# One transformer block on one core: memory rows four to a partition, the router's two halves stacked, and pieces of work put in other places

## The chip, the cores and the metric

The kernel runs on one core of a Trainium2 chip. The metric is the device time of one execution in microseconds (us). Shown are the median, lowest and highest of three executions, and one further execution that the hardware profiler recorded.

## The reference

2048 tokens (32 sequences of 64) of 256 features pass through a gated cross-attention and then a gated mixture of 8 experts with a shared expert.

```python
x = x + tanh(g_xattn) * xattn(layernorm(x), ctx, wq, wk, wv, wo)   # keys and values: [ctx, x], 64 + 64 rows per sequence
x = x + tanh(g_ffn) * ffn(layernorm(x))

def ffn(x):
    probs = softmax(x @ gate_w.T)                    # 8 experts
    top_p, top_i = top_k(probs, 2)                   # combine[n, e] = top_p where chosen, else 0
    h = silu(x @ expert_fc1[e].T) * (x @ expert_fc2[e].T)         # 176 wide, for every expert e
    y = sum_e combine[n, e] * (h @ expert_proj[e].T)
    s = silu(x @ shared_fc1.T) * (x @ shared_fc2.T)               # 704 wide
    return y + sigmoid(x @ shared_gate_w.T) * (s @ shared_proj.T)
```

## The kernel before, in words

TensorE, VectorE, ScalarE, GpSimd and the sync engine (PE, DVE, ACT, POOL and SP in the rows) each run one instruction stream in the order in which the program is written; semaphores tie them together. An engine that waits for one semaphore holds up everything behind it. Nothing but the written order sets the order of the work.

Precision: each float32 value v is kept as a rounded part "hi" (written by ScalarE, line 807, helper `copy`) and a remainder "lo" (VectorE, line 1060 or 1098, helpers `sub` and `scalar_tensor_tensor`); GpSimd makes the lo parts of some loaded data (lines 1554, 1591). A product is three matmuls: hi·hi, hi·lo and lo·hi (`THREE`, helper `chain`, line 424).

Stage by stage:

1. **Attention, chunks c = 0 to 3** of 512 tokens, each in four tiles j of 128. TensorE transposes the normed rows (`first_norm`, L432), makes queries and keys (`project(c, i)`, i = 0..3), `scores(c, j)`, `values(c, j)`, transposes the softmax (`probs_t`, L509) and multiplies (`attend(c, j)`). While chunk c is worked on, TensorE also projects chunk c+1 and norms, transposes and routes chunk c-1: `second_norm`, `router` (logits for 8 experts and the shared gate: 6 matmuls with 72 columns of weights and 512 tokens, rows "router_hi", "router_lo"), `logits` (four small transposes, L552). VectorE does `row_max`, `v_lo`, `probs_lo`, `residual` (L1131, L1135), `aggregate` (L1141) and, two chunks behind, the routing: `two_best`, `counts`, `slots` (L1222 to L1227: which slot of its expert each token takes). `route(c-2)` (L567) is the TensorE product that `slots` reads, in PSUM bank 7. In chunks 2 and 3 `slots(c-2)` stands on VectorE between `residual(c, 0)` and `v_lo(c, 1)`.
2. GpSimd `scatter(c, i)` (L1564, L1568) writes each token's normed row, in groups of 128, to its two slots in memory (`xs_d`); it also computes the reciprocal deviations (`rstd1`, `rstd2`) and the lo parts of the shared weights, after which SP loads the next piece.
3. **Shared expert** in blocks `fc(s, j)` and `pj(s, j)` (L689), s = chunk, j = 0..5. PRE = 3 chunks run before the routed experts, the last chunk after them. VectorE scales each chunk's result by its gate (`s_sums`, L1437) into the tile SX2, and SP stores it in memory (`y2_d`). The last chunk's result is added to the output by L1440.
4. **Routed experts**, 39 slot tiles of 128 rows: `e_step(s, u, m)`, 2 us each. TensorE transposes (L740, L784) and multiplies; GpSimd adds each tile's rows to their tokens' rows in `y2_d` with an indirect, accumulating DMA (L1608).
5. **Combine** (L1402): SP reads the two sums of every token back from `y2_d` (L403, eight loads of 512 KB into the tile called ew_hi), VectorE adds them, SP and ScalarE store the output.

At the start SP issues, in this order: x of chunk 0, the attention weights (3 loads), the context `ctx_t[0]`, x of chunk 1; then, once GpSimd has made the lo part of the context (`cached_lo(0)`, L1554), the next context, constants, and x of chunk 2 (L293). On ScalarE `cached_hi(0)`, which waits for the context, stands ahead of `weight_hi(2)`, `weight_hi(3)`, `project_hi(0, ..)` and `first_apply(1)` (L839), and this last waits for GpSimd's `rstd1(1)`, which stands behind `cached_lo(0)`. VectorE's `ln1_stats(c)` (L1071) waits for x of chunk c; `ln1_stats(2)` stands ahead of `v_lo(0, 0)`. TensorE runs 18 transposes of a constant whose results nobody reads (`warm`, L579), once the constants have come (`d_const`).

## Time and profile before

| | |
|---|---|
| three executions: median (lowest to highest) | 299.07 us (297.09 to 299.75) |
| the profiled execution: its time, its span | 299.84 us, 298.03 us (the page shows 298.0) |
| busy: TensorE, VectorE, ScalarE, GpSimd | 276.6, 215.6, 170.2, 130.3 us |
| chain that ended last | TensorE 59%, VectorE 19%, issue 8%, ScalarE 7%, DMA 4% |
| mean granted TensorE clock | 0.990 of 2.4 GHz |

The busy time of TensorE counts pipelined matmuls up to their modelled ends, so neighbours overlap: the starts in the timeline tell more than the durations. Brackets at the end of a row give the idle time of its engine just before it and what ended that. The chain of waits goes from the last instruction back to what released each step; work that stands in it can't be made longer without a later end.

### The profile page before, as it was taken

How to read it: one execution, taken by the hardware profiler on the slowest of the kernel's cores; microseconds unless marked ns; L12 is line 12 of the kernel's file. 1: busy time of each engine (PE TensorE's matmuls, PEld its weight loads, DVE VectorE, ACT ScalarE, POOL GpSimd, SP SyncE). 2: the span in 40 equal slices, each digit the busy share in tenths (PEclk: the TensorE clock that was granted, in tenths of full speed). 3: DMA queues.
4: the chain of work that ended last, by engine and by line, in shares of the span. 5: the costliest groups of instructions: out<-in, count | busy, mean ns of one | idle time of the engine just before them, and what ended most of it. 6: DMA issues, size and time to landing. Idle time of an engine off the chain costs nothing.

```text
span 298.0 us, 5868 instructions
## 1 busy us (share of the span) xinstructions
PE 276.6 (93%) x1785; PEld 247.8 (83%) x1785; DVE 215.6 (72%) x700; ACT 170.2 (57%) x399; POOL 130.3 (44%) x157
## 2 busy tenths in 40 slices
PE   4988899999999899999999999799999999999991
PEld 3877789789779587798788888699999999998881
DVE  6667776879869748767776767877777787763285
ACT  2766678687566347574235455366676667654230
POOL 2330831542784525445550000057777787775000
PEclk9999999999999799999999999999999999999998
DMA  7470244221135202544415654358888888856796
GB/s 212 164 244 9 71 133 152 70 74 53 47 96 221 79 34 73 187 129 142 142 62 176 218 183 143 108 105 139 132 141 135 141 133 141 119 68 70 257 354 236
DMA packets 30654, 40.18 MB, mean 135 GB/s; under 512 B 2976, under 2 KB 26656, under 8 KB 30624
## 3 DMA queue, kind: packets, MB, share of 16 engines
q1 hardware_dynamic: 22480, 29.53, 31.5%
q0 software_dynamic: 7152, 9.57, 19.5%
q10 hardware_dynamic: 992, 0.71, 0.8%
q8 instruction: 15, 0.25, 0.4%
q14 instruction: 15, 0.12, 0.1%
HBM read 22.68 MB, written 17.11 MB: 134 GB/s over the span
## 4 chain that ended last, share of the span: by engine, by line
PE 59%; DVE 19%; issue 8%; ACT 7%; DMA 4%; POOL 1%; SPq 0%; DVEq 0%; ACTq 0%; POOLq 0%
PE bank L424 45%; PE bank L689 7%; DVE ew_lo L1060 4%; DMA xn_all<-x_dram 3%; ACT ew_hi L807 3%; PE bank L784 3%; PE bank L740 3%; DVE xt_lo L1060 2%; DVE work L1415 2%; DVE neg_max L1108 2%; ACT sh_hi L807 1%; DMA weight_stage<-ew_dram 1%; ACT work L839 1%; DVE work L1437 1%; DVE ln_stats L1071 1%
## 5 line engine op out<-in xcount | busy, mean ns | idle before, releaser
L1608 POOL DMA_INDIRECT y_d<-work,dest_of_slot x39 | 60.5, 1552 | 57.1 <-DVE dest_of_slot L1461 55.6
L424 PE MATMUL bank<-ew_hi,xt_hi 128*128 (+2 forms) x172 | 53.8, 322 | 1.1 <-DVE xt_lo L1060 0.6
L424 PE MATMUL bank<-ew_lo,xt_hi 128*128 (+2 forms) x172 | 51.8, 301 | 0.0
L424 PE MATMUL bank<-ew_hi,xt_lo 128*128 (+1 forms) x133 | 40.5, 305 | 0.0
L1060 DVE TENSOR_TENSOR xt_lo<-bank,xt_hi 128x256 fp32r<-128x256 f32 (+2 forms) x90 | 35.6, 398 | 2.8 <-ACT xt_hi L807 1.5
L1568 POOL DMA_INDIRECT xs_d<-xn_all,slot_of_pair x32 | 33.0, 1032 | 10.1 <-issue 7.3
L424 PE MATMUL bank<-xt_hi,sw_hi 128*128 128x512 f32 x88 | 34.8, 396 | 0.2 <-issue 0.2
L807 ACT ACTIVATE xt_hi<-bank 128x256 fp32r<-128x256 f32 (+1 forms) x90 | 32.8, 409 | 3.4 <-PE bank L784 2.2
L424 PE MATMUL bank<-xt_lo,sw_hi 128*128 128x512 f32 x88 | 34.5, 392 | 0.0
L424 PE MATMUL bank<-xt_hi,sw_lo 128*128 128x512 f32 x88 | 34.3, 390 | 0.0
L1060 DVE TENSOR_TENSOR ew_lo<-bank,ew_hi 128x512 fp32r<-128x512 f32 (+1 forms) x41 | 22.7, 582 | 15.9 <-ACT ew_hi L807 13.8
L424 PEld LDWEIGHTS bank<-ew_hi,xt_hi 128*128 128x128 f32 (+1 forms) x172 | 32.5, 189 | 1.8 <-issue 0.9
L424 PE MATMUL bank<-ew_hi 128*128 128x256 f32 (+1 forms) x100 | 30.9, 315 | 3.2 <-DVE ew_lo L1060 1.8
L424 PEld LDWEIGHTS bank<-ew_lo,xt_hi 128*128 128x128 f32 (+1 forms) x172 | 32.8, 191 | 0.2
L424 PE MATMUL bank<-ew_hi,ew_lo 128*128 128x256 f32 (+1 forms) x100 | 30.6, 312 | 1.5 <-DVE ew_lo L1060 1.5
L807 ACT ACTIVATE sh_hi<-work 128x512 fp32r<-128x512 f32 (+1 forms) x24 | 15.2, 632 | 28.1 <-DVE work L1415 17.9
L424 PE MATMUL bank<-ew_lo,ew_hi 128*128 128x256 f32 (+1 forms) x100 | 30.0, 306 | 1.2 <-DVE ew_lo L1280 0.6
L689 PE MATMUL bank<-sw_hi,sh_hi 128*128 128x256 f32 x96 | 27.1, 288 | 2.2 <-DVE sh_hi L1060 1.9
L807 ACT ACTIVATE ew_hi<-bank 128x512 fp32r<-128x512 f32 (+1 forms) x45 | 21.6, 518 | 9.7 <-PE bank L424 8.2
L689 PE MATMUL bank<-sw_lo,sh_hi 128*128 128x256 f32 x96 | 26.6, 282 | 0.0
L424 PEld LDWEIGHTS bank<-ew_hi,xt_lo 128*128 128x128 f32 x133 | 25.0, 188 | 0.0
L1447 DVE TENSOR_TENSOR work<-work,bank 128x176 f32<-128x176 f32 x39 | 13.1, 337 | 15.5 <-ACT work L1002 15.5
(161 smaller groups left out, 680.9 us busy)
## 6 DMA issues: line engine op xcount, KB each, us to landing
work<-xs_d SPq DMA_DIRECT2D x39, 136.0 KB
weight_stage<-ew_dram SPq DMA_DIRECT2D x10, 486.5 KB, 3.8
ew_hi<-y_d SPq DMA_DIRECT2D x8, 512.0 KB, 7.4
y_d<-work SPq DMA_DIRECT2D x6, 512.0 KB, 3.7
work<-ctx_t_dram SPq DMA_DIRECT2D x4, 512.0 KB, 3.6
xn_all<-x_dram SPq DMA_DIRECT2D x3, 512.0 KB, 6.4
xs_d<-pad_row SPq DMA_DIRECT2D x9, 136.0 KB, 1.9
weight_stage<-sw_dram SPq DMA_DIRECT2D x3, 384.0 KB
```

The lines of the kernel that those rows point to most:

```text
L424: last = nc.tensor.matmul(dst, a, b, start=(n == 0), stop=(n == len(pairs) - 1))
L689: last = nc.tensor.matmul(B[4 + t][:, 0:D], h[:, t * P:(t + 1) * P], w, start=(j == 0 and n == 0), stop=(j == S_FULL and n == len(parts) - 1))
L740: last = nc.tensor.transpose(rows_bank(n)[:, k * P:(k + 1) * P], EX[:, w, k * P:(k + 1) * P], ident)
L784: last = nc.tensor.transpose(B[4 + v][:, i * P:(i + 1) * P], EH[:, v, i * P:(i + 1) * P], ident)
L807: return nc.scalar.activation(dst, src, ACT.Copy, scale=scale)
L839: nc.scalar.activation(XA[:, j, :], XNR[:, c * TPC + j, :], ACT.Identity, bias=nb1[:, j:j + 1], scale=rs1[:, j:j + 1]).then_inc(a_xn, 1)
L1060: return nc.vector.tensor_tensor(dst, src, hi.bitcast(F32), ALU.subtract)
L1108: last = nc.vector.tensor_reduce(nmx[r, j % 2:j % 2 + 1], own_keys(B[4 + j % 2], b), mybir.AxisListType.XY, ALU.max, negate=True)
L1415: nc.vector.tensor_tensor(SHF[0:rows, j % 2, :], STH[0:rows, j % 2, :], h2, ALU.mult).then_inc(v_h, 1)
L1447: nc.vector.tensor_tensor(EH[:, u % 2, 0:F_E], ETH[:, u % 2, :], B[2 + u % 2][:, F_E:2 * F_E], ALU.mult)
L1568: nc.gpsimd.indirect_dma_start(out=xs_d, out_offset=bass.IndirectOffsetOnAxis(ap=POS[:, i, n:n + 1], axis=0), in_=XN[:, n, :], in_offset=N ...
L1608: nc.gpsimd.indirect_dma_start(out=y2_d, out_offset=bass.IndirectOffsetOnAxis(ap=IX[:, n:n + 1], axis=0), in_=EY[:, n % 4, :], in_offset=None,
```

## The change

- **Rows in memory.** The sums in `y2_d` lie four tokens to a partition (token row = 512 c + 4 p + j), so a partition's four rows are one stretch of 4 KB; the slots' destinations (the table `C_TOK`) follow.
- **Router.** Hi and lo weights stand side by side in one tile `router` (columns 0 to 8 and 32 to 40), so one pass gives both products: 4 matmuls instead of 6, with lo·lo added. The logits are transposed with 41 rows instead of 9, and VectorE's copy becomes a sum over the two halves (L1151 before).
- **Routing's slots.** On VectorE `slots(c-2)` goes behind `aggregate(c, 0)`; on TensorE `route(c-2)` goes behind `attend(c, 1)`, into bank 4, and `attend(c, 1)` no longer waits for `v_pos`. On GpSimd `rstd2(c, 0)` goes ahead of the scatter, and the second scatter of chunk 0 into chunk 3.
- **Start.** x of chunk 1 is issued ahead of the context. `ln1_stats(2)` goes behind `row_max(0, 2)`; `project_lo(1, 0)` ahead of `residual(0, 0)`; `project_lo(0, 0)` behind `weight_lo(3)`. The 18 empty transposes become 30 empty matmuls of 64 columns, of which 22 wait only for the memset of `pad_row`.
- **Chunk 1.** `scores(1, 0)` stands between the two halves of `first_norm(2)`. **Chunk 2.** `project(3, 3)` stands ahead of `attend(2, 2)`, on VectorE alike.
- **Before the expert steps.** Of the four products of `s_sums(2)` VectorE does the first ahead of the steps and the second within step 0; ScalarE does the third and fourth within step 0.
- **Last chunk.** `fc(3, 5)` goes ahead of `pj(3, 3)`; `combine(5)` between `s_mult(3, 5)` and `s_lo(3, 5)`, `combine(4)` likewise in block 4. Four of the eight loads from `y2_d` are issued by ScalarE.

```diff
-        y2_t = y2_d[0:TOP * N_TOK, :].rearrange("(i c j p) d -> i c p j d", i=TOP, c=N_CH, j=TPC)
+        y2_t = y2_d[0:TOP * N_TOK, :].rearrange("(i c p j) d -> i c p j d", i=TOP, c=N_CH, j=TPC)
...
-        RW = [sb(f"router_{s}", [P, KD, RW_COLS], F32R) for s in ("hi", "lo")]
+        RW = sb("router", [P, KD, RW_COLS], F32R)
...
+            load_x(1)
             sp.dma_start(CR, ctx_t[0]).then_inc(d_ct, 16)
-            load_x(1)
...
-                sp.wait_ge(v_z, 4 * s + 4)
+                sp.wait_ge(v_z, 4 * s + 4 if s < PRE - 1 else 4 * s + 2)
+                if s == PRE - 1:
+                    sp.wait_ge(a_z, 2)
...
             for c in LAST_FIRST:
-                for i in range(TOP):
-                    sp.dma_start(Y2[i][:, c * TPC:(c + 1) * TPC, :], y2_t[i, c]).then_inc(d_y[i][c], 16)
...
+                    if c > 2:
+                        waits += [(0, v_pos, c - 2)]
...
-                if j == 1 and c > 1:
-                    waits = waits + [(0, v_pos, c - 1)]
...
-                             [(RW[a][:, k, :], XT[b][:, c, k, :]) for k in range(KD) for a, b in THREE], waits)
+                             [(RW[:, k, :], XT[b][:, c, k, :]) for k in range(KD) for b in range(2)], waits)
...
-                    last = nc.tensor.transpose(B[7][:, j * 16:j * 16 + N_E + 1], LGT[:, j * P:(j + 1) * P],
-                                               ident[0:N_E + 1, 0:N_E + 1])
+                    last = nc.tensor.transpose(B[7][:, j * 2 * RW_LO:j * 2 * RW_LO + RW_ROWS], LGT[:, j * P:(j + 1) * P],
+                                               ident[0:RW_ROWS, 0:RW_ROWS])
...
-                bank, o = (B[1], 0) if c == LAST else (B[7], D)
+                bank, o = (B[1], 0) if c == LAST else (B[7], D) if c == LAST - 1 else (B[4], 0)
...
                 else:
-                    pe.wait_ge(v_x2, 4 * (c + 2))
+                    pe.wait_ge(a_exp, 4 * (c + 2) + 3)
...
                 for _ in range(n):
-                    nc.tensor.transpose(B[5][:, 0:P], ident, ident)
...
 
+            pe.wait_ge(zeroed, 1)
+            warm(22)
             pe.wait_ge(d_const, 16)
-            warm(10)
             first_norm(0, 0)
-            warm(4)
             first_norm(0, 1)
-            warm(4)
...
-                if 0 < c < LAST:
+                if c == 1:
                     first_norm(c + 1, 0)
+                    scores(c, 0)
                     first_norm(c + 1, 1)
-                scores(c, 0)
-                scores(c, 1)
+                    scores(c, 1)
+                else:
+                    if c < LAST:
+                        first_norm(c + 1, 0)
+                        first_norm(c + 1, 1)
+                    scores(c, 0)
+                    scores(c, 1)
                 values(c, 0)
...
-                if c > 1:
-                    route(c - 2)
...
                 attend(c, 1)
+                if c > 1:
+                    route(c - 2)
...
-                attend(c, 2)
+                if c != LAST - 1:
+                    attend(c, 2)
                 values(c, 3)
                 probs_t(c, 3)
                 if c < LAST:
                     project(c + 1, 3)
-                else:
+                if c == LAST - 1:
+                    attend(c, 2)
+                if c == LAST:
...
+                    if (s, j) == (PRE - 1, S_FULL) and t < TPC - 1:
+                        last.then_inc(p_pre, 1)
...
-                if s == 1:
-                    pe.wait_ge(v_z, 4 * PRE)
+                if s in (1, 2):
+                    pe.wait_ge(v_z, 4 * (PRE - 1) + s)
+                if s in (2, 3):
+                    pe.wait_ge(a_z, s - 1)
...
-            blocks(PRE, N_CH, 1)
+            fc(LAST, 1)
+            for j in range(2, S_BLK):
+                if j < S_FULL:
+                    pj(LAST, j - 2)
+                fc(LAST, j)
+            for j in range(S_FULL - 2, S_BLK):
+                pj(LAST, j)
...
+                if s == 0:
+                    act.wait_ge(d_z, 16 * (PRE - 1))
+                    for t in (2, 3):
+                        T = (PRE - 1) * TPC + t
+                        if t == 2:
+                            act.wait_ge(p_pre, 3)
+                        else:
+                            act.wait_ge(p_pj, 6 * PRE)
+                        copy(SX2[:, t, :], B[4 + t][:, 0:D], scale=GS[:, T:T + 1]).then_inc(a_z, 1)
...
+                s_hi(LAST, j)
+                if j == 1:
+                    for r in range(4):
+                        act.wait_ge(d_ey[r], 16 * len(range(r, SLOT_TILES, 4)))
+                if j in (1, 2):
+                    for c in LAST_FIRST[2 * j - 2:2 * j]:
+                        act.dma_start(Y2[1][:, c * TPC:(c + 1) * TPC, :], y2_t[1, c]).then_inc(d_y[1][c], 16)
             at = (LAST - 1) * TPC + 2
...
-                nc.vector.tensor_copy(LG[:, c * TPC:(c + 1) * TPC, :],
-                                      B[7][:, 0:TPC * 16].rearrange("p (j n) -> p j n", j=TPC)[:, :, 0:N_E + 1]).then_inc(v_lg, 1)
+                both = B[7][:, 0:TPC * 2 * RW_LO].rearrange("p (j x n) -> p j n x", j=TPC, x=2)[:, :, 0:N_E + 1, :]
+                nc.vector.reduce_sum(LG[:, c * TPC:(c + 1) * TPC, :], both, AX_X).then_inc(v_lg, 1)
...
-            project_lo(0, 0)
             weight_lo(2)
             weight_lo(3)
+            project_lo(0, 0)
...
 
             row_max(0, 0)
...
+            ln1_stats(2)
             v_lo(0, 1)
             probs_lo(0, 1)
+            project_lo(1, 0)
             residual(0, 0)
-            project_lo(1, 0)
...
-                if c > 1:
-                    slots(c - 2)
                 v_lo(c, 1)
...
                 aggregate(c, 0)
                 if c + 2 < N_CH:
                     ln1_stats(c + 2)
+                if c > 1:
+                    slots(c - 2)
...
-                residual(c, 2)
+                if c != LAST - 1:
+                    residual(c, 2)
                 v_lo(c, 3)
                 probs_lo(c, 3)
                 if c < LAST:
                     project_lo(c + 1, 3)
+                if c == LAST - 1:
+                    residual(c, 2)
                 residual(c, 3)
                 aggregate(c, 1)
...
+                if s == 0:
+                    dve.wait_ge(p_pre, 2)
+                    s_sum(PRE - 1, 1)
...
-            s_sums(PRE - 1)
+            dve.wait_ge(d_z, 16 * (PRE - 1))
+            dve.wait_ge(p_pre, 1)
+            s_sum(PRE - 1, 0)
...
+                    combine((0, 4, 5)[j - 3])
                 s_lo(LAST, j)
                 if j == 3:
                     combine(1)
                     combine(2)
                     combine(3)
-                if j == 4:
-                    combine(4)
-                    combine(5)
-                if j == 5:
-                    combine(6)
-                    combine(7)
-            s_sums(LAST)
+            combine(6)
+            combine(7)
+            for t in range(TPC):
+                s_last(t)
...
+                if c == LAST:
+                    scatter(c - 3, 1)
+                rstd2(c, 0)
                 if c > 1:
                     scatter(c - 2, 0)
-                rstd2(c, 0)
...
-                if 1 < c < LAST:
-                    scatter(c - 2, 1)
...
-    rw[:, :, :N_E + 1] = rows(np.concatenate([a["L0_ffn_gate_w"], a["L0_ffn_shared_gate_w"]], 0))
+    rw[:, :, :N_E + 1] = rw[:, :, RW_LO:RW_ROWS] = rows(np.concatenate([a["L0_ffn_gate_w"], a["L0_ffn_shared_gate_w"]], 0))
...
-    consts[:, C_TOK:C_DUM] = np.arange(TOP * N_T)[None, :] * P + np.arange(P)[:, None]
+    tile = np.arange(TOP * N_T)
+    consts[:, C_TOK:C_DUM] = (tile // TPC * CH + tile % TPC)[None, :] + np.arange(P)[:, None] * TPC
```

VectorE in chunk 2, before. The first `v_lo`/`probs_lo` pair for tile 1 is the two rows `ew_lo<-bank,ew_hi` with a_v and a_pt; the rows with v_route are `slots(0)`.

```order
L1135 BN_STATS ln_stats<-work 128x6 [waits v_x2]
L1222 TENSOR_TENSOR work<-work,bank 128x32 [waits p_route]
L1223 TENSOR_REDUCE work<-work 128x4 [waits v_route]
L1222 TENSOR_TENSOR work<-work,bank 128x32 [waits v_route]
L1223 TENSOR_REDUCE work<-work 128x4 [waits v_route]
L1224 TENSOR_SCALAR payload<-work,tanh_gates 128x4x2 [waits v_route]
L1225 SCALAR_TENSOR_TENSOR slot_of_pair<-work 128x2x4 [waits v_route]
L1227 COPY work<-work 128x8 [waits v_route]
L1060 TENSOR_TENSOR ew_lo<-bank,ew_hi 128x512 [waits a_v]
L1060 TENSOR_TENSOR xt_lo<-bank,xt_hi 128x2x256 [waits a_x2t]
L1060 TENSOR_TENSOR ew_lo<-bank,ew_hi 128x256 [waits a_pt]
```

The same place after the change (the lines are those of the changed file), up to `slots(0)`:

```order
L1174 BN_STATS ln_stats<-work 128x6 [waits v_x2]
L1099 TENSOR_TENSOR ew_lo<-bank,ew_hi 128x512 [waits a_v]
L1099 TENSOR_TENSOR xt_lo<-bank,xt_hi 128x2x256 [waits a_x2t]
L1099 TENSOR_TENSOR ew_lo<-bank,ew_hi 128x256 [waits a_pt]
L1137 SCALAR_TENSOR_TENSOR sh_lo<-bank,sh_hi 128x512 [waits a_qk]
L1147 TENSOR_REDUCE neg_max<-bank 64x1 [waits p_sc]
L1147 TENSOR_REDUCE neg_max<-bank 64x1
L1170 SCALAR_TENSOR_TENSOR work<-bank,softmax_scale,xn_all 128x256 [waits p_av]
L1174 BN_STATS ln_stats<-work 128x6 [waits v_x2]
L1180 BN_AGGR ln_mean_var<-ln_stats 128x2 [waits g_rs2,v_st2]
L1180 BN_AGGR ln_mean_var<-ln_stats 128x2
L1261 TENSOR_TENSOR work<-work,bank 128x32 [waits p_route]
```

The three remainders that TensorE's `attend(2, 1)` needs now stand ahead of the seven instructions of `slots(0)`.

VectorE around the first expert step, before: all four products of `s_sums(2)` (banks 4 to 7) stand ahead of step 0's product (L1447).

```order
L1461 TENSOR_SCALAR dest_of_slot<-work,consts_sb 128x1
L1437 TENSOR_SCALAR work<-bank4,shared_gate 128x256 [waits d_z,p_pj]
L1437 TENSOR_SCALAR work<-bank5,shared_gate 128x256
L1437 TENSOR_SCALAR work<-bank6,shared_gate 128x256
L1437 TENSOR_SCALAR work<-bank7,shared_gate 128x256
L1447 TENSOR_TENSOR work<-work,bank2 128x176 [waits e_th]
L1448 TENSOR_TENSOR work<-work,bank2 128x48
```

And after the change:

```order
L1507 TENSOR_SCALAR dest_of_slot<-work,consts_sb 128x1
L1473 TENSOR_SCALAR work<-bank4,shared_gate 128x256 [waits p_pre,d_z]
L1493 TENSOR_TENSOR work<-work,bank2 128x176 [waits e_th]
L1494 TENSOR_TENSOR work<-work,bank2 128x48
L1099 TENSOR_TENSOR xt_lo<-bank0,xt_hi 128x2x128 [waits e_xh]
L1506 COPY weight_of_slot<-work 128x1
L1507 TENSOR_SCALAR dest_of_slot<-work,consts_sb 128x1
L1473 TENSOR_SCALAR work<-bank5,shared_gate 128x256 [waits p_pre]
```

Banks 6 and 7 have left VectorE, and one product is left ahead of step 0's.

## Rows read from the trace of the kernel before

**Rows 1.** The page: TensorE's busy tenths and granted clock in 40 slices.

```profile
PE   4988899999999899999999999799999999999991
PEclk9999999999999799999999999999999999999998
```

**Rows 2.** Timeline of ScalarE at the start: start us, us, engine, line, tiles, idle before.

```profile
11.30 1.06 ACT L807 ACTIVATE ew_hi<-work 128x1024 fp32r<-128x1024 f32 x1 [0.81 <-DMA work<-ctx_t_dram]
17.94 1.09 ACT L839 ACTIVATE work<-xn_all,ln_bias,ln_rstd 128x256 f32<-128x256 f32 x2 [1.44 <-POOL ln_bias L1528]
```

**Rows 3.** Timeline of VectorE at the start.

```profile
12.63 1.41 DVE L1071 BATCH_NORM_STATS2 ln_stats<-xn_all 128x6 f32<-128x256 f32 x4 [1.34 <-DMA xn_all<-x_dram]
```

**Rows 4.** Timeline of TensorE in chunk 0.

```profile
20.29 0.39 PE L424 MATMUL bank<-ew_hi 128*128 128x256 f32 x1 [0.28 <-DVE ew_lo L1060]
...
25.26 0.38 PE L424 MATMUL bank<-ew_hi 128*128 128x256 f32 x1 [1.28 <-DVE ew_lo L1060]
...
31.55 0.50 PE L424 MATMUL bank<-xt_hi,ew_hi 128*128 128x512 f32 x1 [0.90 <-DVE sh_lo L1098]
```

**Rows 5.** Timeline of TensorE, chunk 2: stall, two router matmuls, `logits`.

```profile
78.53 0.39 PE L424 MATMUL bank<-ew_hi,ew_lo 128*128 128x256 f32 x1 [0.54 <-DVE ew_lo L1060]
...
79.34 0.39 PE L424 MATMUL bank<-xt_lo,router_hi 128*72 128x512 f32 x1
79.57 0.39 PE L424 MATMUL bank<-xt_hi,router_lo 128*72 128x512 f32 x1
...
82.22 0.41 PE L552 MATMUL bank<-consts_sb,work 9*128 9x9 f32 x4
```

**Rows 6.** The chain that ended last, in order of time: `slots(0)`, first and last pieces.

```profile
75.42 0.10 DVE work L1222
...
76.78 0.17 DVE work L1227
```

**Rows 7.** Timeline of VectorE behind `aggregate(2, 0)` and `aggregate(3, 0)`.

```profile
82.73 1.02 DVE L1060 TENSOR_TENSOR ew_lo<-bank,ew_hi 128x512 fp32r<-128x512 f32 x2 [1.90 <-issue]
...
106.63 1.02 DVE L1060 TENSOR_TENSOR ew_lo<-bank,ew_hi 128x512 fp32r<-128x512 f32 x2 [3.51 <-ACT ew_hi L807]
```

**Rows 8.** Timeline of TensorE, chunk 3: the same stretch as rows 5.

```profile
99.43 0.35 PE L424 MATMUL bank<-ew_hi 128*128 128x256 f32 x1 [0.74 <-DVE work L1227]
100.85 0.39 PE L424 MATMUL bank<-ew_hi,ew_lo 128*128 128x256 f32 x1 [0.54 <-DVE ew_lo L1060]
106.11 0.41 PE L552 MATMUL bank<-consts_sb,work 9*128 9x9 f32 x4
```

**Rows 9.** Windows: PE, PEld, DVE, ACT, POOL busy, clock, DMA share, GB/s.

```profile
100.00:101.00 1.00, 0.46 (x2) 0.26 (x3) 0.99 (x3) 0.00 (x0) 0.88 (x1) 1.00 0.00 0
102.00:103.00 1.00, 1.00 (x4) 0.54 (x3) 0.93 (x4) 0.25 (x2) 0.69 (x2) 0.50 0.38 134
```

**Rows 10.** Timeline at the first expert steps, VectorE and TensorE.

```profile
189.44 1.66 DVE L1437 TENSOR_SCALAR work<-bank,shared_gate 128x256 f32<-128x256 f32 x4 [0.73 <-PE bank L689]
191.60 0.41 PE L784 MATMUL bank<-consts_sb,work 128*128 128x128 f32 x2 [1.02 <-DVE work L1448]
194.13 0.37 PE L424 MATMUL bank<-ew_hi,xt_hi 128*128 x1
```

**Rows 11.** Groups of instructions: busy us, mean ns of one, idle before.

```profile
L1608 POOL DMA_INDIRECT y_d<-work,dest_of_slot x39 | 60.5, 1552 | 57.1 <-DVE dest_of_slot L1461 55.6
L1568 POOL DMA_INDIRECT xs_d<-xn_all,slot_of_pair x32 | 33.0, 1032 | 10.1 <-issue 7.3
```

**Rows 12.** Timeline of VectorE and TensorE in the last chunk.

```profile
286.30 0.28 PE L689 MATMUL bank<-sw_hi,sh_hi 128*128 128x256 f32 x1
287.73 0.40 PE L424 MATMUL bank<-xt_hi,sw_hi 128*128 128x512 f32 x1
289.12 1.29 DVE L1402 TENSOR_TENSOR xn_all<-ew_hi 128x512 f32<-128x512 f32 x2
292.66 0.36 PE L689 MATMUL bank<-sw_hi,sh_hi 128*128 128x256 f32 x1 [1.95 <-DVE sh_hi L1060]
```

More of the change, by code:

```diff
@@ L578, in warm @@
                 for _ in range(n):
-                    nc.tensor.transpose(B[5][:, 0:P], ident, ident)
+                    nc.tensor.matmul(B[5][:, 0:SEQ], PADROW[:, 0:P], PADROW[:, 0:SEQ], start=True, stop=True)
             def fc(s, j, halves=(0, 1)):
@@ L711, in _, with blocks @@
             pe.wait_ge(sw_lo, SW_PIECES)
-            def blocks(s0, s1, ahead):
-                order = [(s, j) for s in range(s0, s1) for j in range(S_BLK)]
+            def blocks(ahead):
+                order = [(s, j) for s in range(PRE) for j in range(S_BLK)]
                 for n in range(ahead, len(order) + 2):
-                    if n == len(order) and s1 == PRE:
+                    if n == len(order):
                         pe.wait_ge(v_h, 6 * PRE - 1)
@@ L925, in _ @@
             act.wait_ge(d_rw, 16)
-            copy(RW[0][:], RWF[:]).then_inc(rw_hi, 1)
+            copy(RW[:], RWF[:]).then_inc(rw_hi, 1)
             v_hi(0, 2)
```

61 lines of the change are left out of this document (33 added, 28 removed).

## The prediction

> **What bounds the kernel now.** I read the page first, then the chain of waits, then TensorE's timeline for the places where it stands still, and last the timelines of the engines that it waits for there. The page shows TensorE at nine tenths or ten in nearly all slices; the first is at 4, and its clock is full in every slice but the 14th [rows 1]. So an end can only move if TensorE gets less to do or stands still less. From the start of the shared expert (about 110 us) to 184 us and through the 39 expert steps it is never without work for more than some tenths, and the edits leave these stretches alone. What can be won lies at four places: the start, chunks 2 and 3, the first two expert steps, and the last chunk.
>
> **Start, part 1: a loss.** Today the context lands at 11.30, when ScalarE's `cached_hi(0)` has waited for it [rows 2], and x of chunk 1 at 12.63 [rows 3]. They are of one size and change places in SP's queue, so the context should come at about 12.6, 1.3 us late. Behind it on ScalarE stand `weight_hi(2)`, `weight_hi(3)` and the four `project_hi(0)`, and on GpSimd `cached_lo(0)` and `rstd1(1)`; ScalarE's `first_apply(1)`, now at 17.94 and released by GpSimd [rows 2], goes to about 19.2. The copy of the product of the value and output weights, which stands between its halves, and so TensorE's `values(0, 0)`, now at 20.29, go to about 21.3 [rows 4]. The earlier empty matmuls (at 1.3 instead of 4.2 us) and the shorter ones between the transposes let `project(0, 0)` begin a little sooner, but this chain through GpSimd doesn't care.
>
> **Start, part 2: a gain.** `ln1_stats(2)` no longer stands ahead of `v_lo(0, 0)`, which takes away the wait of 1.28 us at 25.26, and `project_lo(1, 0)` ahead of `residual(0, 0)` the one of 0.90 at 31.55 [rows 4]. Sum: 2.2 gained, 1.3 lost, and about 0.3 lost again because ScalarE's `exps(0, 3)` is next on the path. I take 0.6 us; the ends are a loss of 1.3 (the swap alone) and a gain of 2.2 (the swap hidden).
>
> **Router.** A router matmul follows the last by 0.23 us (79.34 to 79.57) [rows 5]. Two fewer for each of four chunks: 8 x 0.23 = 1.84 us of TensorE's own time, all at places where it is the bound or soon becomes it. The transposes grow from 9 to 41 rows and VectorE's copy to a sum over two halves; neither form stands in the trace. Four transposes lie in the 0.41 us of the row at 82.22 [rows 5]; between nothing and double that, so 0 to 1.6 in all, I take 0.2, since their columns are still few. Net 1.6 us.
>
> **Routing's slots.** The chain that ended last runs through all of `slots(0)`, from 75.42 to 76.95, 1.5 us [rows 6], and likewise through `slots(1)`, whose last piece (L1227) releases TensorE at 99.43 [rows 8]. Behind them TensorE also waits at 78.53 and at 100.85 [rows 5, 8]. The new place lies behind `aggregate(c, 0)`, where VectorE today stands idle for 1.90 and 3.51 us [rows 7]: that idle time is the cover, and with the shift both places still have it. If it were gone, `v_lo(c, 2)` would come late by up to 1.5. In chunk 2 TensorE was short of work for about 1.3 us around 77 to 78.5, so 1.2 of the 1.5 are kept (bounds 0 and 1.5). In chunk 3 it is 1.5, and more: after a thin stretch (TensorE busy 0.46 of the us from 100 to 101) the granted clock falls to 0.50, the 1.2 GHz level [rows 9]. From the last stall to `logits` chunk 2 takes 82.22 - 78.53 = 3.69 us, chunk 3, with the same matmuls, 106.11 - 100.85 = 5.26 [rows 5, 8]: the fall costs 1.57. In chunk 2 a shorter stall of the same kind brings no fall, and with the slots gone chunk 3 looks like chunk 2, so I take back the whole 1.57 (bounds 0 and 1.57). Together 1.2 + 1.5 + 1.6 = 4.3 us.
>
> What is queued behind the moved pieces: on GpSimd `scatter(0, 0)` now runs ahead of the lo part of the third shared weight piece, for which SP waits before it loads the tail and, behind that, stores chunk 2's rows. The scatter, four issues of 1.03 us and the gaps between [rows 11], can't begin before `slots(0)` ends, which stands in the gap that begins at 80.83 (82.73 less 1.90) and not at 75.42, some 4 us later after the shift, so the load slips by 2 to 3 us against its surroundings, the store's landing with it; `residual(3, 0)` waits for that landing and has about as much room. I take 0, the bound is a loss of 1.
>
> **Chunk 1 and chunk 2 orders.** `scores(1, 0)` between the transposes fills a TensorE wait, but ScalarE's chain (`first_apply`, `second_apply`, `first_hi`) is behind it and isn't shortened; the wait turns up later. `project(3, 3)` ahead of `attend(2, 2)` likewise: VectorE has the same work before `row_max(3, 0)`. 0 for both (bounds -0.3 and +0.8 each, the sizes of single stalls in rows 4 and 8).
>
> **First expert steps.** VectorE's four products take 1.66 us from 189.44, and step 0's product comes behind them; TensorE waits 1.02 us until 191.60, and its first expert projection is at 194.13 [rows 10]. After the change: one product of 0.4 us, which can start when the first of four banks is ready, then step 0's product at about 189.2; TensorE's transposes follow `up(1)`, which leaves it free at 190.58 (191.60 less 1.02), without a wait, and the projection of step 0 comes at about 192.5. 1.65 us gained. ScalarE's two products delay its `silu` of step 1 by 0.3, behind which is still slack. Ends 0.6 and 2.2. The rows' adder on GpSimd waits for SP's store of these sums, which is no earlier than before; it has 0.45 us in each 2 us step to catch up.
>
> **Last chunk.** TensorE stands still for 1.95 us until 292.66, waiting for the last block's hidden rows, VectorE having done two combines of 1.29 together first; VectorE then has the four output products still ahead of it. `fc(3, 5)` now comes ahead of `pj(3, 3)`, which takes TensorE from 286.30 to 287.73 [rows 12], so 1.43 us sooner, and one combine slips into VectorE's idle gap. So `s_lo(3, 5)` is done some 1.4 us sooner, and the rest with it. The output stores must still pass the DMA queues, so I take 1.3 (bounds 0.5 and 1.9).
>
> **Rows four to a partition.** Nothing waits long for these stores and loads now, and the expert loop's adds go row by row as before: 0. Below nothing is possible; see the last rival.
>
> **Sum.** 0.6 + 1.6 + 4.3 + 1.65 + 1.3 = 9.45 us. The profiled execution took 299.84 (span 298.03 and 1.8 around it): 290.4. The median of the runs shown is 0.8 lower, 299.07, which by the same sum gives 289.6. I forecast 290.0 us. A measurement of this kernel tells about 1% (3 us) from no change.
>
> **Rivals.**
> - *The clock falls at the start.* With the context late, TensorE has nothing to do for about 1.9 us between `scores(0, 1)` and `values(0, 0)`. For it: chunk 3 shows a fall after a thin stretch [rows 9]. Against it: neither the 1.28 at 25.26 [rows 4] nor the 1.95 at 292.66 [rows 12] is followed by one at once. Price: 1.6 for the fall (as in chunk 3) and the 0.6 that the start was to bring: 292.2 us. The Trainium skill, in "TensorE: Matmul & The Clock Gate", section "A second HAM failure mode: psum-queue depth-cycling", says that many short pauses between groups of matmuls can make the clock fall too, without one long pause. Rows 9 agree with it; rows 4 show pauses without a fall.
> - *The slots' gain is only moved.* VectorE is full in chunks 2 and 3; if the moved slots push `v_lo(c, 2)` back, or the late store holds `residual(3, 0)`, half of the 4.3 and 1 us more go: 293.2. For it: VectorE is idle just there only because it waits for TensorE. Against: the 1.90 and 3.51 of rows 7.
> - *The expert weights' loads set the time, not TensorE.* Then all that is won before 184 us is lost in a wait before the first step, and only 1.65 + 1.3 remain: 296.9. Against it: the loads are released by conversions that go with the blocks, and the page shows TensorE at work in nearly every slice before [rows 1].
> - *The rows' adder becomes the bound: slower.* Slots of one tile hold ascending tokens; their rows now lie 4 KB times a whole number apart within a chunk, no longer 1 KB. The adder has 39 instructions of 1.55 us in steps of 2 us [rows 11], and its tile of outputs is free again only when an add four steps back has landed. If adds take so much longer that a step grows from 2.0 to 2.32 us, 39 x 0.32 = 12.5 us come on top: 302.5. It eats the whole gain at 0.24 us a step. For it: nothing in the rows, except that the loop has little slack. Against: each add moves the same 128 rows of 1 KB.
>
> **Chances.** Forecast 0.68; clock 0.12; slots 0.10; weights 0.05; adder 0.05. The forecast's own range, from its bounds, is 287.0 to 292.5. I give 287.0 to 294.5, which takes in the first two rivals. Faster by over 1% (below 296.1): 0.90, within 1%: 0.06, slower: 0.04.
>
> **What would show it.** Right: `slots(0)` and `slots(1)` no longer in the chain; no slice with a lower clock; 4 router matmuls; `values(0, 0)` near 21.3; first expert projection some 2 us sooner after the first transposes; TensorE's last wait below 1 us; a step still of 2.00 us. Wrong: a slice with a lower clock in the first 30 us, a wait of `residual(3, 0)` for a DMA, VectorE busy up to `v_lo(c, 2)` while TensorE waits, or a step above 2.05.

## The result, and where the profile after differs

The changed kernel takes 296.23 us in the median of 20 executions (294.92 to 299.61), the kernel before 298.66 (297.09 to 300.06, 20 executions): a ratio of 0.9936, 95% interval 0.9916 to 0.9956. It is faster by 2.4 us by the medians (0.8%; the ratio says 0.6%), where I had forecast about 9, a time of 290.0 and a range of 287.0 to 294.5. One execution, the 299.61, was over 1.5% slower than the fastest and is left out of the ratio, though not of the median. The profiled execution took 297.94, its span 296.1 for 298.0 before.

The page of the changed kernel, busy tenths and granted clock of TensorE (for [rows 1]): the first slice is now at 8 instead of 4, and the lower clock of the 14th slice is gone.

```profile
PE   8999999999999799999999999999999999999993
PEclk9999999999999999999999999999999999999999
```

TensorE's timeline of the changed kernel: the start (for [rows 4]), and `logits(0)`.

```profile
1.21 9.65 PE L585 MATMUL bank<-pad_row 128*128 128x64 f32 x44 [1.21 <-DVE pad_row L1327]
10.65 1.70 PE L436 MATMUL bank<-consts_sb,work 128*128 128x128 f32 x7
...
12.36 3.51 PE L585 MATMUL bank<-pad_row 128*128 128x64 f32 x16
15.63 1.20 PE L428 MATMUL bank<-ew_hi 128*128 128x512 f32 x2
16.63 1.05 PE L428 MATMUL bank<-ew_hi,ew_lo 128*128 128x512 f32 x2
...
18.99 0.63 PE L428 MATMUL bank<-ew_hi,ew_lo 128*128 128x512 f32 x2
...
61.66 0.44 PE L556 MATMUL bank<-consts_sb,work 41*128 41x41 f32 x4
```

Here the busy share misleads. The 22 empty matmuls ahead of the norm (44 records, two for each) hold TensorE from 1.21 to 10.65, 0.43 us each; only then does the first norm run (6.73 before, in two halves). Eight more stand between it and `project(0, 0)`, which begins at 15.63. TensorE is "busy" all that time with results nobody reads.

The other places, again TensorE's timeline of the changed kernel: chunk 3 (for [rows 8]), the first steps (for [rows 10]), the wait in the last chunk (for [rows 12]).

```profile
84.97 0.44 PE L556 MATMUL bank<-consts_sb,work 41*128 41x41 f32 x4
...
102.33 0.39 PE L428 MATMUL bank<-ew_hi 128*128 128x256 f32 x1 [0.80 <-ACT ew_hi L832]
103.22 0.38 PE L428 MATMUL bank<-ew_hi,ew_lo 128*128 128x256 f32 x1 [0.39 <-DVE ew_lo L1099]
106.86 0.44 PE L556 MATMUL bank<-consts_sb,work 41*128 41x41 f32 x4
...
190.59 0.38 PE L803 MATMUL bank<-consts_sb,work 128*128 128x128 f32 x2
192.05 0.38 PE L803 MATMUL bank<-consts_sb,work 128*128 128x128 f32 x2
194.77 0.38 PE L803 MATMUL bank<-consts_sb,work 128*128 128x128 f32 x2
...
290.76 0.35 PE L704 MATMUL bank<-sw_hi,sh_hi 128*128 128x256 f32 x1 [0.73 <-DVE sh_hi L1099]
```

From the last stall in chunk 3 to `logits(2)` it is 3.64 us now, 5.26 before: no clock fall in this execution. But just before that stretch TensorE now waits 0.80 for ScalarE, where it waited 0.74 for VectorE's slots. The second step follows the first after 1.46, the third that one after 2.72. The last wait is 0.73 for 1.95.

### The profile page after: what moved, and what is told of

Read it like the earlier page. It is cut to its first block, busy times and chain, and to the rows that moved or that the text cites. A ratio compares the mean times of both kernels' runs of the same rounds, so it can differ in the third digit from the quotient of the medians.

```text
span 296.1 us, 5942 instructions
## 1 busy us (share of the span) xinstructions
PE 283.4 (96%) x1819; PEld 256.6 (87%) x1819; DVE 215.3 (73%) x698; ACT 170.6 (58%) x401; POOL 130.9 (44%) x157
## 4 chain that ended last, share of the span: by engine, by line
PE 55%; DVE 23%; ACT 9%; issue 6%; DMA 3%; POOL 2%; SPq 0%; DVEq 0%; ACTq 0%
PE bank L428 38%; PE bank L704 6%; PE bank L585 4%; DVE ew_lo L1099 4%; ACT ew_hi L832 3%; PE bank L803 3%; DVE work L1458 3%; PE bank L757 3%; ACT sh_hi L832 2%; DVE neg_max L1147 2%; DMA y_d<-work 2%; DVE xt_lo L1099 2%; DVE sh_lo L1099 1%; POOL xs_d L1616 1%; ACT work L864 1%
## 5 line engine op out<-in xcount | busy, mean ns | idle before, releaser
L428 PE MATMUL bank<-ew_hi 128*128 128x256 f32 (+1 forms) x100 | 31.5, 322 | 1.5 <-ACT ew_hi L832 1.4
```

Of the source, the lines that this page charges most:

```text
L428: last = nc.tensor.matmul(dst, a, b, start=(n == 0), stop=(n == len(pairs) - 1))
```

## Experiments

A "mark" below is the start of a group on TensorE: logits(0) to logits(3), the third and the last expert step, the last shared product. The distance between two marks tells what one stretch costs, whatever came before it. A ratio is to the kernel before, executed in turn with the kernel of the experiment; its 95% interval stands in brackets.

Each profile also has a record of TensorE's granted clock. Its first entry is not at 0 but where the full clock sets in: at 8.98 us in the kernel before, at 18.73 in the changed one. The rows of the page and of the windows count the time ahead of it as full speed. "The clock rises" below means this first entry; where it falls, the granted clock is 0.50.

### The empty work

**e1: the old empty transposes** (`warm` issues transposes of `ident` again, and its calls go back):

```diff
-            pe.wait_ge(zeroed, 1)
-            warm(22)
             pe.wait_ge(d_const, 16)
+            warm(10)
             first_norm(0, 0)
+            warm(4)
             first_norm(0, 1)
-            warm(8)
+            warm(4)
```

> The changed kernel with the empty work of before: 10, 4 and 4 transposes of a constant, at their old places. Theory A (the 30 empty matmuls are the loss: each takes 0.43 us in two records of 0.22, they hold TensorE from 1.21 to 10.65 and from 12.36 to 15.63 and with it the first norm and the first projection): project(0, 0) starts near 10 us, logits(0) near 58 instead of 61.66, and the whole is 3 to 4 us under the changed kernel, about 292.5 to 293.5. Theory B (the start is late for the context's later load, the empties only fill a wait): project(0, 0) near 10 us too, but values(0, 0) stays near 25, and the time stays within 1 us of 296.2. Theory C (an early start is given back behind chunk 3 by a load or by the loop): logits(0) near 58, first expert step still near 190.6, time within 1 us of 296.2.

293.19 us (292.57 to 293.59, 6 executions), ratio to before 0.9823 [0.9794, 0.9852]: 3.0 under the changed kernel. TensorE's timeline of e1:

```profile
10.06 0.73 PE L428 MATMUL bank<-ew_hi 128*128 128x512 f32 x2 [0.25 <-ACT ew_hi L832]
...
21.10 0.39 PE L428 MATMUL bank<-ew_hi 128*128 128x256 f32 x1 [1.25 <-DVE ew_lo L1099]
...
57.07 0.44 PE L556 MATMUL bank<-consts_sb,work 41*128 41x41 f32 x4
80.39 0.44 PE L556 MATMUL bank<-consts_sb,work 41*128 41x41 f32 x4
...
97.74 0.38 PE L428 MATMUL bank<-ew_hi 128*128 128x256 f32 x1 [0.77 <-ACT ew_hi L832]
98.63 0.38 PE L428 MATMUL bank<-ew_hi,ew_lo 128*128 128x256 f32 x1 [0.39 <-DVE ew_lo L1099]
102.27 0.44 PE L556 MATMUL bank<-consts_sb,work 41*128 41x41 f32 x4
...
187.50 0.38 PE L803 MATMUL bank<-consts_sb,work 128*128 128x128 f32 x2
189.15 0.40 PE L428 MATMUL bank<-ew_hi,xt_hi 128*128 x1 [0.45 <-issue]
...
190.19 0.38 PE L803 MATMUL bank<-consts_sb,work 128*128 128x128 f32 x2
```

logits(0) is at 57.07 for 61.66, and all later marks lie 4.57 to 4.59 earlier as well. Nothing is given back: theory A holds, B and C fall. `values(0, 0)` is at 21.10 (forecast 21.3). The clock rises at 8.65.

**e2: ten empty matmuls, none behind the norm** (`warm(22)` to `warm(10)`, `warm(8)` deleted).

> The changed kernel with 10 empty matmuls ahead of the first norm instead of 22 and none behind it. Theory A (queue): 10 x 0.43 = 4.3 us from 1.21, done at 5.5, so the first norm starts when its data is there (about 7), project(0, 0) near 9.5 to 10; time as e1, 292.5 to 293.5. Rival D (TensorE's rate at the start matters as much as the queue): its matmuls then run at half rate longer, project(0, 0) to project(0, 3) take 1.5 us or more longer than in e1, time 294 to 295.

293.61 us (293.57 to 293.98), 0.9845 [0.9814, 0.9876]. The matmuls of `project(0, 0)`, from 10.60, follow one another at half rate until 14.8 (the clock rises at 14.55), yet logits(0), at 57.42, is only 0.35 behind e1. The queue of empties costs, and rival D is worth some tenths.

**e3: only the new empty work, in the kernel before** (the diff of e1 read backwards, on before).

> The kernel before with the 30 empty matmuls of the change (22 ahead of the first norm, 8 behind) and nothing else of it. Theory A: project(0, 0) near 15.6 and the whole 3 to 5 us slower than before, 302 to 304. Theory B: within 1 us of before, since the other edits of the start make the loss.

301.80 us (300.11 to 302.44), 1.0092 [1.0057, 1.0126]: 3.7 slower by the medians, 2.7 by the ratio; its executions fall into two groups, 300.1 to 300.4 and 301.8 to 302.4. logits(0) is at 62.24 for 58.05. The edit alone does what its removal takes back.

**e5: the changed kernel once more, for its second group.**

> The changed kernel unaltered, for a second profile: its 20 executions lie in two groups, 12 near 295.0 to 296.5 and 8 near 297.5 to 298.0, and the profile at hand (span 296.1) is of the upper one. Theory F (the groups differ by when TensorE's rate doubles at the start): if the execution is of the lower group, the empty matmuls ahead of the first norm end well before 10.65 or project(0, 0) is at full rate from its first matmul, and logits(0) stands 2 to 3 us before 61.66 while all later stretches are as long as before. Theory G (they differ by a clock fall elsewhere or by transfers): logits(0) stays at 61.66 and the difference appears later.

297.06 us. TensorE's timeline, then windows (columns as in [rows 9]), of e5:

```profile
12.36 2.40 PE L585 MATMUL bank<-pad_row 128*128 128x64 f32 x16
14.56 0.71 PE L428 MATMUL bank<-ew_hi 128*128 128x512 f32 x2
...
59.17 0.44 PE L556 MATMUL bank<-consts_sb,work 41*128 41x41 f32 x4
...
100.82 0.39 PE L428 MATMUL bank<-ew_hi,ew_lo 128*128 128x256 f32 x1 [0.47 <-DVE ew_lo L1099]
105.99 0.44 PE L556 MATMUL bank<-consts_sb,work 41*128 41x41 f32 x4
```

```profile
102.00:103.00 1.00, 1.00 (x4) 0.61 (x3) 0.90 (x6) 0.22 (x2) 0.09 (x1) 0.57 0.05 20
103.00:104.00 1.00, 1.00 (x5) 0.90 (x5) 0.86 (x5) 0.57 (x1) 0.92 (x3) 0.50 0.63 242
```

Theory F holds, and a second thing changes from one execution to the next. The first norm is at 10.65 as in the other profile, but the clock rises at 13.40 instead of 18.73: the last empties already run faster and the projection starts at 14.56 at full rate; logits(0) is 2.49 earlier. Then the clock falls in chunk 3 with the slots already moved (100.82 to 105.99 is 5.17 us). The two together fit the list of 20: ten from 294.9 to 295.9, one at 296.55 (clock mean 0.991), eight from 297.5 to 298.1, one at 299.61 (0.991). That the groups differ in these two is shown by the two profiles alone, and fits the rest. Of the 4.59 between e1 and the first profile, 2.1 is thus the queue as it stands at the start's low clock (59.17 - 57.07), and 2.49 is the later rise of the clock, which falls on part of the executions.

**e9: ones (1.5) in place of zeros**, in a tile of their own.

```diff
-                    nc.tensor.matmul(B[5][:, 0:SEQ], PADROW[:, 0:P], PADROW[:, 0:SEQ], start=True, stop=True)
+                    nc.tensor.matmul(B[5][:, 0:SEQ], ONES[:, 0:P], ONES[:, 0:SEQ], start=True, stop=True)
```

> The changed kernel, its 30 empty matmuls on a tile that holds 1.5 everywhere instead of on zeros; count, size and place unchanged. Theory H (the late doubling of TensorE's rate, at about 14.5 or 18.3 us though it had been at work from 1.21, comes from the zeros): the records shrink from 0.22 to 0.11 us within the 22, the first norm starts when its data is there (7 to 8 us) and the time is 292.5 to 294.5. Rival I (what is multiplied doesn't matter): the first norm again at 10.65, two groups near 295 and 297.8, median within 1 us of 296.2.

295.97 us (295.40 to 297.38), 0.9930 [0.9903, 0.9957]; the first norm is at 10.79, the clock rises at 13.56. Theory H falls: 1.5 does no better than 0. (This profile too has a fall of the clock in chunk 3.)

**e14: only the block of 22** (`warm(8)` deleted).

> The changed kernel without its last 8 empty matmuls; the 22 ahead of the first norm stay. They hold project(0, 0) for 8 x 0.43 = 3.4 us by their own length, of which the hi and lo parts of the first norm hide about 1 (in e2 the projection starts 2.7 us after the first norm starts, in the changed kernel 5.0). By the queue theory: first norm at 10.65, project(0, 0) near 13.3, the time 1 to 2.3 us under the changed kernel's 296.2. Rival (the 8 run in a wait for data anyway): project(0, 0) near 15 and the time within 0.5 us of 296.2.

296.18 us (295.46 to 296.85, 10 executions), 0.9929 [0.9904, 0.9954]. Its chain is as I expected and its time is not: `project(0, 0)` starts at 13.25, 1.3 before e5's, but at half rate until about 16 (the clock rises at 16.07), so logits(0) is at 59.15, the same as e5's 59.17. The 8 buy back what they take, in the median; the loss lies with the 22. It has no execution near 297.8.

**e13: no empty work at all** (on e12, below; the calls of `warm` deleted).

> e12 with no empty work of TensorE at all (the 18 transposes of a constant left out). If the empties are worth their place: TensorE's rate doubles later (12 to 18 us instead of about 10), project(0, 0..3) cost 1.5 to 3 us more and the time is 1 to 2.5 us above e12's 291.57. Rival (the start then waits for the weights' and ScalarE's chain, the half rate is covered): within 0.5 us of e12.

292.46 us (291.89 to 293.45), 0.9805 [0.9771, 0.9838], 0.9 above e12. TensorE's timeline of e13 (each row two matmuls):

```profile
7.21 2.03 PE L436 MATMUL bank<-consts_sb,work 128*128 128x128 f32 x8 [7.21 <-DVE work L1122]
9.92 1.22 PE L428 MATMUL bank<-ew_hi 128*128 128x512 f32 x2 [0.69 <-ACT ew_hi L829]
...
12.65 1.05 PE L428 MATMUL bank<-ew_hi 128*128 128x512 f32 x2
13.50 1.05 PE L428 MATMUL bank<-ew_hi,ew_lo 128*128 128x512 f32 x2
...
15.00 0.63 PE L428 MATMUL bank<-ew_hi 128*128 128x512 f32 x2
15.47 0.62 PE L428 MATMUL bank<-ew_hi,ew_lo 128*128 128x512 f32 x2
```

Two matmuls take 0.85 us (12.65 to 13.50) until 14.35, and 0.47 (15.00 to 15.47) from 15.00 on; the clock rises at 14.75, in e12 at 8.39. The old transposes are worth about 0.9 us, a little less than the 1 to 2.5 I had expected. e12 differs from e1 by edits worth 1.6 (293.19 less 291.57); without them e13 would stand near 294.1, so by this estimate no empty work at all is still 2 us better than the changed kernel's 30.

**e10: six empty matmuls in the idle time ahead of the old transposes** (on e7).

```diff
+            pe.wait_ge(zeroed, 1)
+            early(6)
             pe.wait_ge(d_const, 16)
             warm(10)
```

> e7 (transposes of before, context ahead of x of chunk 1) with 6 empty matmuls in the idle time from 1.2 to 3.8 us ahead of the constant's landing. If earlier empty work makes the rate double earlier: project(0, 0) at full rate from its first matmul (e7: half rate until 12.6), the time 0.5 to 1 us under e7's 292.4, and a smaller spread. Rival (the start then waits for the weights and ScalarE anyway, or the rate does not depend on these): within 0.3 us of e7.

292.20 us (291.48 to 292.33), 0.9794 [0.9767, 0.9821]; e7 has 292.40. `project(0, 0)` starts at 10.63 and is at full rate from 11.3 (the clock rises at 10.87, in e7 at 12.36), so earlier work made little of a difference: 0.2 us, which these intervals can't tell from none.

### The moved pieces

**e4: slots and route back** (on e1). On VectorE, with `route` on TensorE ahead of `second_norm(c - 1, 1)`, bank 7 and the old waits likewise:

```diff
                 residual(c, 0)
+                if c > 1:
+                    slots(c - 2)
                 v_lo(c, 1)
...
                     ln1_stats(c + 2)
-                if c > 1:
-                    slots(c - 2)
```

> e1 with slots(c-2) and route(c-2) back at their old places and bank. My forecast's step (slots worth 2.7 by stalls and 1.6 by the clock): 4.3 us slower than e1. By the trace of the changed kernel, where chunk 2's stalls sum to 1.2 for 1.9 before and chunk 3's to 3.5 for 3.7, the stalls were only moved to other waits: 0.4 to 0.7 plus the clock's 1.6 if its fall comes back, so 0.5 to 2.3 us slower than e1, and a slice with a lower clock near 100 us decides between the two ends.

295.98 us (295.47 to 296.94), 0.9919 [0.9889, 0.9950]: 2.8 above e1: less than my forecast's 4.3, more than the 0.5 to 2.3 that I had read from the traces. TensorE's timeline of e4:

```profile
99.08 0.36 PE L428 MATMUL bank<-ew_hi 128*128 128x256 f32 x1 [1.26 <-DVE work L1264]
...
100.51 0.39 PE L428 MATMUL bank<-ew_hi,ew_lo 128*128 128x256 f32 x1 [0.55 <-DVE ew_lo L1097]
...
105.28 0.44 PE L556 MATMUL bank<-consts_sb,work 41*128 41x41 f32 x4
```

Chunk 2 (logits(0) to logits(1)) is 0.60 longer than in e1, chunk 3 is 2.56 longer, of which 1.13 is the slower clock behind the stall (100.51 to 105.28 is 4.77 us, 3.64 in e1). Undone with all else in place, the move is worth more than it brought against the kernel before: there chunk 3's stalls hardly shrank. The slower clock is not the whole of it: the three executions of e4 with a clock mean of 0.995 or 0.996 take 295.47 to 295.63, 2.4 above e1, the three with 0.989 or 0.990 take 296.33 to 296.94. Which other edit makes the old order dearer than it was in the kernel before stays open.

**e6: chunk 2's attend(2, 2) ahead of project(3, 3) again** (on e1).

```diff
-                if c != LAST - 1:
-                    attend(c, 2)
+                attend(c, 2)
...
-                if c == LAST - 1:
-                    attend(c, 2)
```

> e1 with attend(2, 2) and residual(2, 2) back ahead of project(3, 3). My forecast's step: 0 to 0.8 us slower than e1. Rival (the moved projection delays the first attention products, so chunk 3 pays for it by ScalarE's waits at 90.73, 92.58 and 97.74): up to 1 us faster than e1. The stretch from logits(1) to logits(2) is 21.88 us in e1: above 21.9 for the first, near 21 for the second.

293.33 us (292.34 to 293.62), 0.9839 [0.9818, 0.9861]: no difference. In the profile the stretch is 21.57 for 21.88, 0.3 in favour of the old order; the medians don't show it. (VectorE's `residual(2, 2)` goes back with it.)

**e7: the context ahead of x of chunk 1 again** (on e1; the two lines in SP's program change places).

> e1 with the context issued ahead of x of chunk 1 again. My forecast's step (the swap alone loses up to 1.3 us by GpSimd's chain: values(0, 0) is at 21.10 in e1 behind a wait of 1.25): values(0, 0) near 19.9 to 20.3 and the time 0.8 to 1.3 us under e1, near 292. Rival (the swap is hidden: first_apply(1) waits for x of chunk 1 and its statistics as much as for the context): values(0, 0) near 21 and within 0.3 us of e1.

292.40 us (292.22 to 292.75), 0.9812 [0.9794, 0.9829]: 0.8 under e1. TensorE's wait of 1.25 for `values(0, 0)` is gone, and `first_apply(1)` is at 17.91 for 18.75. The swap is a loss, by GpSimd's chain, as forecast.

**e8: the four products on VectorE again** (on e1).

```diff
-            dve.wait_ge(d_z, 16 * (PRE - 1))
-            dve.wait_ge(p_pre, 1)
-            s_sum(PRE - 1, 0)
+            s_sums(PRE - 1)
```

> e1 with the four products of s_sums(2) on VectorE ahead of the steps again, as before. My forecast's step: 1.65 us slower than e1. By e1's trace, where the third step starts 0.69 us late (190.19 - 187.50 = 2.69 for 2.00) behind ScalarE's two products: only 1.3 us slower, with a wait of about 1.0 us of TensorE for VectorE at the first step and none at the third.

294.73 us (294.03 to 294.95), 0.9891 [0.9875, 0.9907]: 1.5 above e1, with the wait of 1.02 at the first step and no late third step behind it.

**e12: ScalarE's second product one step later** (on e7).

```diff
-                if s == 0:
-                    act.wait_ge(d_z, 16 * (PRE - 1))
-                    for t in (2, 3):
+                if s in (0, 1):
+                    if s == 0:
+                        act.wait_ge(d_z, 16 * (PRE - 1))
+                    for t in (2 + s,):
```

> e7 with ScalarE's second product of s_sums(2) one expert step later. If the third step's late start (2.69 instead of 2.00 after the second in e1) comes from ScalarE's two products in one step: 2.3 or less there and 0.3 to 0.6 us under e7's 292.4. Rival (the two short steps before it only moved work forward, the third waits for the loop's own chain): the third step starts at the same distance from the first (4.2 us) and the time stays within 0.2 us of e7.

291.57 us (291.17 to 292.25), 0.9783 [0.9755, 0.9811]: 0.8 under e7 (expected 0.3 to 0.6) and the lowest median of all, 4.7 under the changed kernel. TensorE's timeline of e12:

```profile
186.20 0.38 PE L803 MATMUL bank<-consts_sb,work 128*128 128x128 f32 x2
...
188.21 0.38 PE L803 MATMUL bank<-consts_sb,work 128*128 128x128 f32 x2
```

The third step now follows the second after 2.01; in e1 it was 2.69 (187.50 to 190.19), with a wait of 0.45 at 189.15 that the profile put down to nothing ("issue").

**e11: the rows 128 tokens apart again** (on e7; the two places of the diff that hold the layout).

> e7 with the sums' rows 128 tokens apart again (store, loads and the table of destinations as before). Theory J (the rows four to a partition make each step 0.005 to 0.007 us longer: 2.005 to 2.007 in the changed kernel for 2.000 before): steps of 2.000, 0.2 to 0.3 us less in the loop. Against it stand the smaller packets of the last loads and stores: the end may lose as much, so the time lies within 0.5 us of e7's 292.4. Theory K (the step's length comes from elsewhere): steps of 2.005 again.

292.85 us (291.63 to 294.14), 0.9832 [0.9804, 0.9861]: 0.45 above e7, within their spread. The steps are 2.008 again, so theory K: the layout does not make them. It decides nothing here, as forecast.

**e15: e12 with the old order of chunk 2** (e6's edit).

> e12 with attend(2, 2) back ahead of project(3, 3), the last edit that may cost (e6 against e1: 21.57 for 21.88 us from logits(1) to logits(2), but no difference of the medians). Expected 0 to 0.3 us under e12's 291.57; above 292 it would mean that chunk 3 pays for it elsewhere. It is the candidate for the fastest version.

292.35 us (291.07 to 293.04), 0.9802 [0.9769, 0.9836]. It holds the lowest execution of all and some high ones; three of six have a mean clock of 0.991 or 0.992, none of e12's five. It is no gain.

## Why the prediction was wrong

The marks of before, of e1 (the change without its empty work) and of the changed kernel give the whole account. Each difference is before less e1:

| stretch | before | e1 | gained | forecast |
|---|---|---|---|---|
| to logits(0) | 58.05 | 57.07 | 0.98 | 0.6 + 0.4 (router) |
| chunk 2, to logits(1) | 24.17 | 23.32 | 0.85 | 1.2 + 0.4 |
| chunk 3, to logits(2) | 23.89 | 21.88 | 2.01 | 3.1 + 0.4 |
| to logits(3) | 19.17 | 18.68 | 0.49 | 0.4 |
| to the third step | 70.49 | 69.24 | 1.25 | 1.65 |
| steps, to the last (267.76, e1 262.46) | 71.99 | 72.27 | -0.28 | 0 |
| to the last shared product (293.56, e1 287.09) | 25.80 | 24.63 | 1.17 | 1.3 |
| sum | | | 6.47 | 9.45 |

Against this the changed kernel loses 4.59 at the start, in the profiled execution: 6.47 - 4.59 = 1.9, which is the difference of the spans (298.0 and 296.1).

- **The step that failed** is the sentence of part 1 of the start that the earlier and shorter empty matmuls "let `project(0, 0)` begin a little sooner". I gave 30 instructions no length. I also misread their place: none stands between the halves of the first norm, the last 8 stand behind it, right ahead of `project(0, 0)`. The trace of before has a neighbour: ten empty transposes take 2.40 us, 0.24 each. Even that would have put 22 at 5.3 us, until 6.5, just hidden; measured are 0.43 for each, so the 22 end at 10.65 and the 8 more take 3.3 (12.36 to 15.63). No edit that puts work at the head of a queue may stand in a sum without a duration. The 30 instructions are the difference between e1 and the changed kernel, 3.0 of the 6.2 us by which the median missed 290.0; e1 itself, at 293.19, is 3.2 above it, for the slots and the smaller items below.
- **Start otherwise: right**, 0.98 less the router's 0.46 is 0.5 for 0.6. The swap costs 0.9 by the marks of e7 (57.07 and 56.20), for which I had charged 1.3; in e7's profile the clock rose late (12.36), and e12 and e15, with the same order and a rise at 8.39 and 8.20, have logits(0) at 55.75 and 55.82, which is the 1.3. The rival of a clock that falls at the start did not come.
- **Router: right in size, by the marks.** 2 x 0.23 less for each chunk, 1.84 in all, and the stretch to logits(3), where little else changed, is 0.49 shorter; the wider transposes show next to nothing (0.44 for 0.41). No run takes this edit back alone.
- **Slots: mis-sized, and the second rival in its mild form.** Chunk 2 gained 0.39 beside the router (1.2 forecast), chunk 3 1.55, all of it the clock (e3, with the old order and no fall, needs 22.32 for this stretch, 1.57 less than before): the stalls of chunk 3 that I saw end are taken over by waits for ScalarE (0.77 at 97.74 in e1), which stood just behind. I priced VectorE's cover and did not ask which engine would be late next. e4 shows that undoing the move would still cost 2.8, or 2.4 without a fall.
- **The clock: right in direction, wrong in certainty.** I took the fall as a consequence of the slots' stall, there with it and gone without it. It can come and stay away with either order: e3 has the old order and none (3.70 us from 105.08 to 108.78), e5 the new one and a fall. But the order changes how often. The four profiles with a fall in chunk 3 (before, e4, e5, e9) have a clock mean of 0.990 or 0.991, of which that fall takes 0.006, so an execution at 0.995 or above had none. With the slots at the old place such are 24 of 62 (19 of the 49 executions of the kernel before that went with the experiments, 2 of 7 of e3, 3 of 6 of e4); at the new place 83 of 92. These kernels differ in other edits too; the one comparison by a single edit is e4 with e1, 3 of 6 to 6 of 6. (A mean below 0.995 is no proof of a fall in chunk 3: e3's 0.991 comes from the end.) So the fall is no certain 1.57 to take back but that size times a chance, which a single profile can't tell.
- **First steps: mis-sized,** 1.25 for 1.65. ScalarE's two products did not have the slack that I gave them; e12 shows it, and moving one of them gains 0.8.
- **Last chunk: right**, 1.17 for 1.3, by the marks; no run takes it back alone. **Rows four to a partition and chunk 2's order: right** at about nothing (e11, e6); chunk 1's order has no run of its own. The adder was no bound (a step has grown by 0.008 us at most), and the expert weights weren't either: in e1 the third step comes 5.6 us earlier than before (190.19 for 195.77).
- **The loop** costs 0.28 that I did not see: steps of 2.006 to 2.008 us in every kernel with the change's other edits, 2.000 in before and in e3. It is not the empty work (e1, e3, e13), the slots (e4), chunk 2's order (e6), the swap (e7), the products (e8) or the layout (e11). Which edit it is stays open.
- The median of before, 298.66, lies 1.2 under its profiled execution, and e1's, 293.19, near its own (293.38). So the 6.47 by the marks are 5 to 5.5 by the medians. So a little over half of the 9.45 was real; that the changed kernel kept only 2.4 of it comes from the term that was missing.

## What to carry to other kernels

Empty work put in "idle" time needs a length and an end like any other instruction: multiply a measured neighbour by the count and see what waits behind it in the queue. Here the neighbour, a transpose of another form, would have passed with 0.2 us to spare (6.5 for 6.73) and been wrong by nearly two times; with so thin a margin only a trace of the new form decides. A stall that is removed is worth only the distance to the next late engine, so look for that one's arrival before taking the whole. And where a term rests on the clock of one profiled execution, give it the chance that it has, not its size.

## What the runs showed of the hardware

- An empty float32 matmul of 64 columns leaves two records of 0.22 us (0.43 in all, changed kernel), a transpose of 128 columns one of 0.24 (kernel before): half the columns took nearly twice the time, both at the low clock of the start.
- TensorE starts at its lower clock, and the granted clock of the page does not say so: that row shows full speed from 0 on, while matmuls of 512 columns stand 0.43 us apart, and 0.23 later. Behind the clock's fall in chunk 3 of before, at a granted 0.50, the router's matmuls of the same 512 columns stand 0.43 apart too, so the start runs at the 1.2 GHz level; and the clock's record begins with its rise, at the time at which the matmuls change their pace (14.75 in e13, where they do so between 14.35 and 15.00).

```profile
102.08 0.63 PE L424 MATMUL bank<-xt_lo,router_hi 128*72 128x512 f32 x1
102.51 0.63 PE L424 MATMUL bank<-xt_hi,router_lo 128*72 128x512 f32 x1
```

- The Trainium skill ("TensorE: Matmul & The Clock Gate", section "Wait — 56ns, not 53.3ns?") gives 426.7 and 215.7 ns from start to start for 512 columns at the two levels. The traces agree at the lower one, with 0.43; at the upper one they have 0.23, 8% more.
- The clock rose at 8.1 to 9.6 us in eight of the nine profiles that have the old transposes and nothing ahead of them (before, e1, e4, e6, e8, e11, e12, e15), at 12.36 in the ninth (e7), 10.87 in e10, 14.55 in e2, 14.75 in e13, 16.07 in e14, and at 13.40 (e5), 13.56 (e9), 18.64 (e3) and 18.73 (the changed kernel) with all 30 empty matmuls. Work from 1.21 on did not bring it earlier than work from about 4.2 on did; what decides among these stays open.
- Whether the clock falls in a thin stretch is a matter of the execution: of the two profiles of the changed kernel one has the fall in chunk 3 (e5) and one has not. The place of the slots goes with how often, by the counts above. The wait in the last chunk, 1.95 us in the kernel before, can be followed by one as well: in e3 the clock falls at 295.1, behind that wait, and from the last step to the last shared product it takes 26.45 us for 25.80.
